# Row factors of an attention kernel spread over the partitions by transfers through DRAM instead of by matrix products

## What is computed

```python
h = jnp.einsum('bnd,ade->bane', feat_in, W)            # 12 heads of 32
th = jnp.tanh(h)
attn_src = jnp.einsum('bane,aeo->bano', th, w_src)     # s, one per row and head
attn_dst = jnp.einsum('bane,aeo->bano', th, w_dst)     # d, one per column and head
attn = attn_src + jnp.swapaxes(attn_dst, 2, 3)
attn = jnp.where(attn >= 0, attn, LEAKY_ALPHA * attn)  # 0.2
attn = jnp.where(~adj[:, None], -999.0, attn)
attn = jax.nn.softmax(attn, axis=-1)
feat_out = jnp.einsum('banm,bame->bane', attn, h) + b
feat_out = jax.nn.elu(feat_out)
gate = jax.nn.sigmoid(feat_in @ H_w.T + H_b)
return gate * feat_out + (1.0 - gate) * feat_in
```

## Time and profile before

| | before |
|---|---|
| median of 3 runs | 1105.98 us (1105.11 to 1106.05) |
| the profiled execution | 1105.45 us |
| its span | 1103.6 us |
| PE busy | 1056.6 us (96%), 9199 instructions |
| PEld busy | 895.9 us (81%) |
| DVE busy | 872.9 us (79%), 2289 instructions |
| POOL busy | 703.9 us (64%), 605 instructions |
| ACT busy | 651.4 us (59%), 2060 instructions |
| chain that ended last, by engine | PE 79%, DVE 12%, issue 6%, ACT 1% |
| DMA | 31.00 MB, mean 28 GB/s |

### The profile page before, as it was taken

One profiled execution on the slowest core, in us unless ns is written; L12 is line 12 of the kernel. 1 busy time (PEld: TensorE's weight loads), 2 busy tenths in 40 slices (PEclk: granted clock), 3 DMA queues, 4 the chain that ended last, 5 costly groups with the idle time before them and its releaser, 6 DMA issues.

```text
span 1103.6 us, 28424 instructions
## 1 busy us (share of the span) xinstructions
PE 1056.6 (96%) x9199; PEld 895.9 (81%) x9199; DVE 872.9 (79%) x2289; ACT 651.4 (59%) x2060; POOL 703.9 (64%) x605
## 2 busy tenths in 40 slices
PE   6999999999999999999999999999999999999964
PEld 4888888888888888888888888888888888888753
DVE  3659779696987969789696987969689796978986
ACT  4747466474755647565575746657565564747522
POOL 0347577575757758577574856757576674857764
PEclk9999999999999999999999999999999999999985
DMA  7101010010101001010100101001010100100000
GB/s 188 32 1 33 30 33 15 19 34 21 31 29 31 7 21 31 29 31 20 37 9 21 31 29 31 7 21 31 29 31 29 31 7 21 31 29 2 10 15 36
DMA packets 34722, 31.00 MB, mean 28 GB/s; under 512 B 15872, under 2 KB 34688, under 8 KB 34688
## 3 DMA queue, kind: packets, MB, share of 16 engines
q1 hardware_dynamic: 34688, 30.57, 9.1%
HBM read 17.98 MB, written 12.58 MB: 28 GB/s over the span
## 4 chain that ended last, share of the span: by engine, by line
PE 79%; DVE 12%; issue 6%; ACT 1%; POOL 0%; DMA 0%; DVEq 0%; POOLq 0%; ACTq 0%
PE p_bank L573 50%; PE t_bank L712 5%; PE context L726 5%; DVE weights L1032 4%; PE scores L635 4%; PE context L732 4%; PE t_bank L644 3%; PE context L656 3%; PE t_bank L605 2%; PE t_bank L740 2%; PE t_bank L682 2%; DVE sd L1001 1%; DVE masked L940 1%; DVE neg_max L948 1%; PE t_bank L703 1%
## 5 line engine op out<-in xcount | busy, mean ns | idle before, releaser
L1139 POOL TENSOR_TENSOR w_rows<-qwT,own_head 96x1536 fp32r<-96x1536 f32 x64 | 179.8, 2810 | 87.0 <-ACT qwT L873 87.0
L1032 DVE SCALAR_TENSOR_TENSOR weights<-t_bank,pqw,clip 128x128 f32<-128x128 f32 x768 | 206.4, 344 | 7.4 <-PE t_bank L712 6.6
L1132 POOL TENSOR_TENSOR prod<-th,w_sd 128x768 f32<-128x768 f32 x64 | 118.2, 1846 | 124.8 <-ACT th L836 124.7
L808 ACT ACTIVATE probs<-masked,neg_max 128x128 f32<-128x128 f32 x384 | 148.8, 391 | 46.4 <-DVE neg_max L948 46.4
L573 PE MATMUL p_bank<-xT,w_q 128*128 128x512 f32 x432 | 113.6, 408 | 4.3 <-DVE w_k L917 4.3
L573 PE MATMUL p_bank<-w_v,xT 128*128 128x384 f32 x576 | 115.2, 344 | 1.2 <-DVE clip L985 1.2
L573 PE MATMUL p_bank<-w_f,cT 128*128 128x384 f32 x576 | 115.4, 344 | 0.4 <-DVE cT L910 0.4
L573 PE MATMUL p_bank<-w_h,x1T 128*128 128x384 f32 x576 | 114.0, 343 | 0.2 <-DVE x1T L910 0.2
L573 PE MATMUL p_bank<-w_g,x1T 128*128 128x384 f32 x576 | 113.9, 342 | 0.0
L573 PE MATMUL p_bank<-xT,w_k 128*128 128x512 f32 x432 | 111.5, 402 | 0.0
L1120 POOL TENSOR_TENSOR probs<-probs,rden 128x768 f32<-128x768 f32 x64 | 94.3, 1473 | 25.2 <-DVE rden L953 25.2
(11 more groups left out here) (107 smaller groups left out, 2314.7 us busy)
## 6 DMA issues: line engine op xcount, KB each, us to landing
x_in<-in_x_dram SPq DMA_DIRECT2D x16, 768.0 KB, 4.7
out_dram<-y_out SPq DMA_DIRECT2D x64, 192.0 KB, 1.9
adj_in<-in_adj_dram SPq DMA_DIRECT2D x16, 64.0 KB, 4.3
probs0T<-in_L_gnn_Wq_dram SPq DMA_DIRECT2D x1, 576.0 KB, 5.7
weights<-in_L_gnn_Wk_dram SPq DMA_DIRECT2D x1, 576.0 KB, 6.8
x_res<-in_L_gnn_Wv_dram SPq DMA_DIRECT2D x1, 576.0 KB, 7.3
probs<-in_L_gnn_Wf_dram SPq DMA_DIRECT2D x1, 576.0 KB, 7.7
x<-in_L_gnn_W_dram SPq DMA_DIRECT2D x3, 192.0 KB, 6.1
```

What stands on the lines that cost most here:

```text
L808: last = act.activation(probs0[:, k % 2, b, j * P:(j + 1) * P], masked[:, k % 2, b * PAIRS + j, :], ACT.Exp, bias=neg_max[:, b * PAIRS + j ...
L1032: last = dve.scalar_tensor_tensor(out=weights[:, g % 2, n, :], in0=src[:, i * P:(i + 1) * P], scalar=pqw[:, g % 2, 0, n:n + 1], in1=clip[: ...
L1132: pool.tensor_tensor(prod[:], over_heads(th[:], 2), w_sd[:], ALU.mult).then_inc(s_prod, 1)
L1139: pool.tensor_tensor(w_rows[0:QW_ROWS, k % 2], over_heads(qwT[:, k % 2, 1, :].bitcast(F32), H1), per_head(own_head[:], P), ALU.mult).then_ ...
```

## The change

`qwhi`, `qwlo`, `qwT`, `qwTo` and `wb` go, and with them `qw_parts`, `qwT`, `own_head` and `w_rows`. ACT writes w to `w_exp` [128, 2, 12]. SP gets a list of its own with four kinds of steps. `keep` writes w_exp of a graph to a scratch in DRAM as [head, row]: 1536 words of 4 bytes, each its own piece, since neighbours in DRAM lie on different partitions. `spread` reads the scratch, 6 KB, once for each of the 128 partitions into `w_spread` [128, 12, 128]. Both are double buffered. `rows` on POOL now multiplies w_spread by q in place, and `e` reads w_spread instead of a PSUM bank. `load` and `store` are the other two kinds of steps on SP; load comes behind the first spread of a turn, the stores behind the last. PE is left with 22 instead of 38 uses of its transpose banks a turn. All lists of all engines are new in their order.

The diff, without most of the lists and the semaphores' declarations:

```diff
 PE_LOOP = [
-    ("v", 0), ("x1T", 0), ("qk", 0), ("x1T", 1), ("qk", 1), ("qk", 2), ("h", 0), ("gate", 0), ("qk", 3), ("h", 1),
-    ("qwT", 0), ("qk", 4), ("x1T", 2), ("qk", 5), ("gate", 1), ("s", 0), ("qwT", 1), ("wb", 0), ("v", 1), ("wb", 1),
-    ("s", 1), ("wb", 2), ("h", 2), ("wb", 3), ("wb", 4), ("pv1", 0), ("wb", 5), ("gate", 2), ("x1T", 3), ("sumsT", 0),
-    ("pv1", 1), ("h", 3), ("pT", 0), ("s", 2), ("pT", 1), ("pT", 2), ("pT", 3), ("pv0", 0), ("s", 3), ("qwT", 2),
-    ("sumsT", 1), ("v", 2), ("qwT", 3), ("f", 0), ("wb", 6), ("wb", 7), ("v", 3), ("wb", 8), ("pv0", 1), ("pT", 4),
-    ("pT", 5), ("wb", 9), ("wb", 10), ("pv1", 2), ("wb", 11), ("f", 1), ("sumsT", 2), ("pv0", 2), ("pT", 6),
-    ("maskT", 0), ("pv1", 3), ("maskT", 1), ("pT", 7), ("f", 2), ("sumsT", 3), ("pv0", 3), ("xT", 0), ("gate", 3),
-    ("xT", 1), ("f", 3), ("xT", 2), ("xT", 3),
+    ("qk", 0), ("qk", 1), ("x1T", 0), ("v", 0), ("qk", 2), ("x1T", 1), ("h", 0), ("gate", 0), ("x1T", 2), ("qk", 3),
+    ("h", 1), ("qk", 4), ("qk", 5), ("gate", 1), ("s", 0), ("v", 1), ("s", 1), ("h", 2), ("s", 2), ("gate", 2),
+    ("pv1", 0), ("x1T", 3), ("sumsT", 0), ("v", 2), ("pT", 0), ("pT", 1), ("h", 3), ("pv0", 0), ("pv1", 1), ("s", 3),
+    ("maskT", 0), ("v", 3), ("pT", 2), ("pT", 3), ("f", 0), ("xT", 0), ("pv0", 1), ("sumsT", 1), ("gate", 3),
+    ("pT", 4), ("pT", 5), ("f", 1), ("pv0", 2), ("xT", 1), ("pv1", 2), ("pT", 6), ("sumsT", 2), ("pT", 7), ("f", 2),
+    ("pv0", 3), ("xT", 2), ("xT", 3), ("pv1", 3), ("maskT", 1), ("sumsT", 3), ("f", 3),
 ]
...
 DVE_LOOP = [
-    ("x1lo", 0), ("gsum", 0), ("x1lo", 1), ("sd", 0), ("sda", 0), ("wlog", 0), ("qwlo", 0), ("sd", 1), ("sda", 1),
-    ("wlog", 1), ("qwlo", 1), ("gsum", 1), ("x1lo", 2), ("mask", 0), ("e", 0), ("max", 0), ("e", 1), ("e", 2),
-    ("mask", 1), ("e", 3), ("e", 4), ("e", 5), ("rden0", 0), ("max", 1), ("rden1", 0), ("x1lo", 3), ("f_raw", 0),
-    ("sd", 2), ("sda", 2), ("rden0", 1), ("wlog", 2), ("gsum", 2), ("mask", 2), ("max", 2), ("sd", 3), ("sda", 3),
-    ("qwlo", 2), ("wlog", 3), ("mixa", 0), ("mixb", 0), ("qwlo", 3), ("sum1", 0), ("rden1", 1), ("clo", 0),
-    ("stats1", 0), ("mask", 3), ("mv1", 0), ("rden0", 2), ("f_raw", 1), ("max", 3), ("e", 6), ("e", 7), ("e", 8),
...
+    ("x1lo", 0), ("gsum", 0), ("x1lo", 1), ("sd", 0), ("sda", 0), ("wlog", 0), ("sd", 1), ("sda", 1), ("wlog", 1),
+    ("gsum", 1), ("x1lo", 2), ("mask", 0), ("max", 0), ("mask", 1), ("e", 0), ("e", 1), ("e", 2), ("max", 1),
+    ("gsum", 2), ("sd", 2), ("rden0", 0), ("sda", 2), ("e", 3), ("rden1", 0), ("x1lo", 3), ("f_raw", 0), ("wlog", 2),
+    ("e", 4), ("rden0", 1), ("e", 5), ("mask", 2), ("max", 2), ("clo", 0), ("mixa", 0), ("mixb", 0), ("sum1", 0),
+    ("clip", 0), ("sd", 3), ("sda", 3), ("wlog", 3), ("rden0", 2), ("mask", 3), ("stats1", 0), ("max", 3),
+    ("sum0", 0), ("stats0", 0), ("mv1", 0), ("xlo", 0), ("mv0", 0), ("rden1", 1), ("clo", 1), ("f_raw", 1), ("e", 6),
...
 POOL_LOOP = [
-    ("prod", 0), ("prod", 1), ("rows", 0), ("rows", 1), ("x_res", 0), ("prod", 2), ("norm", 0), ("fb", 0),
-    ("norm", 1), ("prod", 3), ("ex", 0), ("rows", 2), ("norm", 2), ("rows", 3), ("fb", 1), ("norm", 3), ("ex", 1),
-    ("rstd1", 0), ("rstd0", 0), ("fb", 2), ("ex", 2), ("rstd0", 1), ("fb", 3), ("rstd1", 1), ("rstd0", 2), ("ex", 3),
-    ("rstd1", 2), ("rstd0", 3), ("rstd1", 3),
+    ("x_res", 0), ("prod", 0), ("prod", 1), ("rows", 0), ("prod", 2), ("rows", 1), ("norm", 0), ("fb", 0),
+    ("norm", 1), ("ex", 0), ("prod", 3), ("norm", 2), ("rows", 2), ("fb", 1), ("norm", 3), ("ex", 1), ("rows", 3),
+    ("rstd1", 0), ("rstd0", 0), ("fb", 2), ("ex", 2), ("rstd0", 1), ("rstd1", 1), ("fb", 3), ("rstd0", 2), ("ex", 3),
+    ("rstd0", 3), ("rstd1", 2), ("rstd1", 3),
 ]
...
+SP_LOOP = [
+    ("keep", 0), ("spread", 0), ("load", 0), ("keep", 1), ("spread", 1), ("keep", 2), ("spread", 2), ("keep", 3),
+    ("spread", 3), ("store", 0), ("store", 1), ("store", 2), ("store", 3),
+]
...
-SHIFT = {n: 2 for n in ("xT", "xhi", "xlo")} | {n: 1 for n in (
+SHIFT = {n: 2 for n in ("xT", "xhi", "xlo", "load")} | {n: 1 for n in (
...
-        pqw = sb("pqw", [P, 2, 3, H1])
-
-
-        qw_parts = sb("qw_parts", [P, 2, 2, QW_ROWS], F32R)
-        qwT = sb("qwT", [QW_ROWS, 2, 2, P], F32R)
-        own_head = sb("own_head", [QW_ROWS, H1])
-        w_rows = sb("w_rows", [P, 2, H1, P], F32R)
+        pq = sb("pq", [P, 2, 2, H1])
+
+
+        w_exp = sb("w_exp", [P, 2, H1])
+        w_kept = [nc.dram_tensor(f"w_kept{i}", [H1, P], F32, kind="Internal").ap() for i in range(2)]
+        w_spread = sb("w_spread", [P, 2, H1, P])
         weights = sb("weights", [P, 2, H1, P])
...
-            def load(t):
-                first = at(t * GROUP)
-
-                sp.wait_ge(pe["xT"], upto(t, GROUP, 0))
-                sp.wait_ge(s_xb, upto(t, 1, 0))
-                sp.wait_ge(s_adjb, upto(t, 1, 0))
-                sp.sem_inc(s_free, 1)
-                sp.dma_start(x_in[:], x_dram[:, bass.ds(first, GROUP), :]).then_inc(s_x, 16)
-                sp.dma_start(adj_in[:], adj_dram[:, bass.ds(first, GROUP), :]).then_inc(s_adj, 16)
-
-            def store(t):
-                for g in range(GROUP):
-                    graph = at(t * GROUP + g)
-                    sp.wait_ge(s_y, upto(t, GROUP, g + 1))
+            def step(name, k, g1, turn):
+                if name == "load":
+                    t = g1 + 2
+                    first = at(t * GROUP)
+
+                    sp.wait_ge(pe["xT"], upto(t, GROUP, 0))
+                    sp.wait_ge(s_xb, upto(t, 1, 0))
+                    sp.wait_ge(s_adjb, upto(t, 1, 0))
+                    sp.sem_inc(s_free, 1)
+                    sp.dma_start(x_in[:], x_dram[:, bass.ds(first, GROUP), :]).then_inc(s_x, 16)
+                    sp.dma_start(adj_in[:], adj_dram[:, bass.ds(first, GROUP), :]).then_inc(s_adj, 16)
+                elif name == "keep":
+
+                    sp.wait_ge(s_pqw, upto(g1, 3 * GROUP, 3 * k + 3))
+                    sp.sem_inc(s_spread_free, 1)
+
+                    wait(sp, s_wspread[k % 2], upto(g1, GROUP // 2 * 16, k // 2 * 16))
+                    sp.sem_inc(s_spread_free, 1)
+                    sp.dma_start(w_kept[k % 2].rearrange("h i -> i h"), w_exp[:, k % 2, :],
+                                 allow_slow_non_contiguous=True).then_inc(s_kept[k % 2], 16)
+                elif name == "spread":
+
+                    sp.wait_ge(s_kept[k % 2], upto(g1, GROUP // 2 * 16, (k // 2 + 1) * 16))
+                    sp.sem_inc(s_spread_free, 1)
+
+                    wait(sp, s_e, upto(g1, THIRDS * GROUP, THIRDS * (k - 1)))
+                    sp.sem_inc(s_spread_free, 1)
+                    sp.dma_start(w_spread[:, k % 2].rearrange("p h i -> p (h i)"),
+                                 w_kept[k % 2].rearrange("h i -> (h i)").partition_broadcast(P)
+                                 ).then_inc(s_wspread[k % 2], 16)
+                elif name == "store":
+                    graph = at(g1 * GROUP + k)
+                    sp.wait_ge(s_y, upto(g1, GROUP, k + 1))
                     sp.dma_start(out_dram[:, bass.ds(graph, 1), :],
-                                 y_out[:, g % 2, :].unsqueeze(1)).then_inc(s_store[g % 2], 16)
-
-            load(1)
-            load(2)
-            store(0)
-            with sp.Fori(1, NG - 2) as u:
-                load(u + 2)
-                store(u)
-            store(NG - 2)
-            store(NG - 1)
+                                 y_out[:, k % 2, :].unsqueeze(1)).then_inc(s_store[k % 2], 16)
+
+            phases(sp, step, "SP", NG)
             for g in range(2):
...
-                elif name == "qwT":
-
-                    te.wait_ge(s_qwlo, upto(g1, GROUP, k + 1))
-                    dst = bank(t_bank, t_freed, name, k, g1, turn)
-                    for i in range(2):
-                        last = te.transpose(dst[0:QW_ROWS, i * P:(i + 1) * P], qw_parts[:, k % 2, i, :].bitcast(F32),
-                                            ident[:])
-                    last.then_inc(pe["qwT"], 1)
-                elif name == "wb":
-
-                    g, r = divmod(k, THIRDS)
-                    te.wait_ge(s_rows, upto(g1, GROUP, g + 1))
-                    dst = bank(t_bank, t_freed, name, k, g1, turn)
-                    heads = slice(H1 // THIRDS * r, H1 // THIRDS * (r + 1))
-                    te.matmul(dst[:, :], qwT[:, g % 2, 0, :],
-                              w_rows[0:QW_ROWS, g % 2, heads, :].rearrange("p h i -> p (h i)"),
-                              start=True, stop=True).then_inc(pe["wb"], 1)
                 elif name == "pv1":
...
-                    wait(act, s_qwlo, upto(g1, GROUP, k - 1))
-                    act.activation(pqw[:, k % 2, 0, :], sda[:, 1, :], ACT.Exp).then_inc(s_pqw, 1)
-                    act.activation(pqw[:, k % 2, 1, :], sda[:, 1, :], ACT.Exp, scale=LEAKY).then_inc(s_pqw, 1)
+                    wait(act, s_prod1, upto(g1, GROUP, k - 1))
```

(54 more changed lines are left out.)

187 lines of the change are left out of this document (90 added, 97 removed), and 107 rows, old and new, of tables (DVE_BEGIN, DVE_END, DVE_LOOP, PE_BEGIN).

## The result

The changed kernel takes 1638.01 us (1628.96 to 1640.78, four runs) against 1105.55 us (1102.65 to 1106.05, four runs) of the kernel before: 1.481 times as long, 95% interval 1.4745 to 1.4875. The forecast was 1066, the range 1022 to 1122; even the case of slow transfers ended at 1132. The profiled run took 1640.78 us.

The account below looks back on a forecast made before the run. PE was taken to bound the loop: 65.8 us a turn less 5.4, plus 2.5 waiting, gives p = 62.9. With 242.0 for begin and end, 1029 + 15 (p - 60.4) gave 1066 us, range 1022 to 1122.

Parts of the forecast that it names:

- the case of slow transfers: Rival: keep and spread at their upper ends, 12.2 us together, turn 64.5, 1091 us, a loss above 13.2; chance 0.12.
- PE's loss of work, 60.4 us a turn: PE in the loop sheds 12 broadcasts (4.2 us) and 8 transposes (1.2), so its turn falls from 65.8 to 60.4 us.
- the case that all hides: Rival: transfers and port cost nothing, PE alone sets the turn at 60.4 us, 1029 us in all; chance 0.22.
- the open L: Begin and end: the transfer latency lies open in the last graph's chain, adding 5 us, for 242.0 in all.
- e at its old price: DVE's e, reading w_spread in SBUF instead of PSUM, stays at 12.8 us a turn.
- rows 2.8, spread 4.7: POOL's rows takes 2.8 us as before; the spread lands in 4.7 us, ends 3.9 and 6.1.
- keep 2.8, ends 1.9 and 6.1: The store of 1536 4-byte words lands in 2.8 us: fixed part about 1.4 plus 1.4 for the pieces.
- L once a turn: Latency from w's exponential to w on all partitions, 7.5 us, ends 5.8 and 12.2; up to about 8 little is lost.
- turn = 52.3 + L: Turn length once the latency from w's exponential to w on all partitions exceeds about 8 us.
- Load behind spread 0 is free: SP's load of x_in behind the first spread costs nothing, as x_in is wanted 25 us later.
- The port, 2.5 us on POOL: POOL's prod 2 waits for e 2 at the SBUF port; PE waits 2.5 us a turn at pT 0, 2.0 for the port.
- DVE pays: Rival: DVE stands still for POOL's operations, 12.8 us a turn, turn 66.6, 1122 us, slower; chance 0.16. Sign: e's mean longer.

Follow-up runs that it names:

- 18: Kernel after without keep and spread, e reading one constant SBUF tile, rows and x_res both cut to 12 columns: 1085.99 us (0.9836).
- 11: Kernel after without keep and spread, e reading one constant SBUF tile, rows cut to 12 columns: 1153.77 us.
- 10: Kernel after without keep and spread, rows multiplying a constant SBUF tile by q, e on one SBUF input: 1201.95 us (1.0895).
- 5: Kernel after without keep, spreads reading a scratch filled once, e as a reduction with one SBUF input: 1221.41 us (1.1055).
- 6: Kernel after with keep, e as a reduction with one SBUF input: 1598.10 us (1.4468).
- 2: Kernel after without keep, spreads reading a scratch filled once, e still on two SBUF inputs: 1416.92 us.
- 7: Kernel after with keep's 1536 words written 512 bytes apart, spreads reading another scratch filled once: 1364.62 us.
- 4: Kernel before with all of e reading a constant SBUF tile instead of PSUM: 1312.57 us (1.1887).
- 9: Kernel before with the middle one of each graph's three e steps reading a constant SBUF tile instead of PSUM: 1285.22 us (1.1649).
- 14: Kernel before with POOL's x_res moved in the loop from behind rows 1 to the head of its list: 1129.31 us (1.024).
- 1: Kernel after with scratch as [row, head], so keep writes 128 pieces of 48 bytes; rows and e read in 48-byte steps: 1478.39 us (1.3381).
- 16: Kernel after with SP issuing keeps in pairs, the second before the wait for the first to land: 1820.03 us (1.6494).
- 13: Kernel after without keep and spread, e on one SBUF input, x_res moved in the loop to behind prod 1: 1205.38 us (1.0914).

## Why the prediction was wrong, step by step

The sum of the prediction, 1066 us, is fast for four reasons: the keep was sized at 2.8 us and took 11.5; its latency was counted once a turn and stands three times in the chain; the port was charged to POOL and is paid by DVE; and the new place of x_res was not priced at all. The runs add up so: 1086 (18), with x_res 1154 (11), with rows 1202 (10), with the spread 1221 (5), with the keep 1598 (6), with e's second input 1638. The last two steps depend on their order: e's second input costs 196 us without a keep (2 and 5) and 40 with one.

- **PE's loss of work, 60.4 us a turn.** PE's own work came out near: busy 985 us in 18, forecast 970, and in its loop, from 500 to 600 us, 93.66 of 100 us at clock 1.00, which makes 61.0 us a turn. But no run came near the case that all hides, 1029: with even rows and x_res cut a turn is 65.1, and mix is still slowed in it. Whether 60.4 could be had without any fight for the port, no run shows. I had laid out the new order's path for one graph and took the rest as PE-bound. Begin and end went from 248 to 338 us; in 18, with no transfers, they take 237, which is what the sum had before its 5 for the open L.
- **e at its old price.** When POOL doesn't shut it out it costs less, 271 ns at the shortest against a mean of 344 before; with a mean of 511 this doesn't come to bear.
- **rows 2.8, spread 4.7**: 2.79 and 4.4. Right; 6.7 where the next keep is issued 1 us behind the spread, and 4.0 in 5, without keeps.
- **keep 2.8, ends 1.9 and 6.1**: 11.5 us. The term that failed worst. The rate of W's 1536 pieces is one of reads from DRAM, of 128 bytes each; I used it for writes of 4 bytes. The split of a store's 1.9 us that gave its fixed 1.4 is in no row either. The pieces do pass the engines within 2 us; the 9.5 us behind are in no row of before. The bound should have stayed open upwards, as the trace had no row of a small write. The Trainium skill (DMA: Bandwidth & Descriptors, Specifications) has a read-modify-write under 512 B. 7 against the kernel after shows that size alone is not it, since as many words of the same size, with room between them, land in 3.4 us.
- **L once a turn.** "SP is taken for 4 L, no queue grows" and "turn = 52.3 + L" failed. L is on the path three times for keep and twice for spread, by SP's order and by wlog 2 behind e 3. With the measured L = 15.9 the formula gives a turn of 68.2 and 1146 us; the turn is 100.1 and the time 1638. So the wrong size of the keep alone explains 80 of the 572 us by which the forecast was missed; the rest is in how often it counts, in the port and in x_res.
- **Load behind spread 0 is free**: no. The load's two issues, 1.4 us, stand in the chain before keep 1; keep 1, beside it, takes 12.5 us in place of 11.2; and x_in lands in 9.3 in place of 4.7.
- **The port, 2.5 us on POOL.** POOL's means did not move (prod 1854 ns, norm 1479), and e's rose to 511: the sign that I named for "DVE pays". That rival had the mechanism right. Its 12.8 us of work for DVE came near by luck (12.3 in 4), since its working, by shares, fails in 9; and it still took the time too low, as DVE's free time hid none of it in 4. I had left out that a DVE operation with one SBUF input is shut out too (y_out, wlog, x). The Trainium skill says it in the section I quoted (SBUF — State Buffer, Who interferes with whom): a `tensor_scalar` can use both port pairs, a `tensor_reduce` never contends. The traces agree: y_out 3.55 us, wlog 2.66, while the reductions sd and neg_max keep their 936 to 948 ns in the runs after as before. Its rule is that whoever issues first blocks the other. With pieces of 0.3 us on DVE and 1 to 3.5 on POOL, it would cost POOL little even if both waited as often; but in 9 DVE doesn't get in between two POOL operations either, and why is not shown.
- **Not in the sum at all**: x_res at the head of POOL's list (68 us between 18 and 11), though the diff shows it, and PE's clock. The same 8879 instructions keep PE busy 985 us at 0.988 (18), 1014 at 0.962 (10), 1123 at 0.85 (after). So a kernel in which PE waits long pays for it again in PE's clock; the short waits of 14 left the clock at 0.99.

## What to carry to other kernels

Before a product on PE is replaced by transfers, look for a row of just such a transfer, direction, piece and neighbourhood in DRAM; without one leave its bound open, and follow the chain through all graphs of a turn, counting how often the latency stands in it. When an operand moves from PSUM to SBUF, list every POOL operation that can be running or queued there; here the queue set the price, not the share of busy time, and moving one POOL operation only slowed other steps in its place. A list's order is part of the change even for steps that keep their work.

## What the runs showed of the hardware

- 1536 words of 4 bytes written next to each other in DRAM land 11.2 to 12.5 us after issue (medians of graphs 0 and 1), 768 of them in 9.1 to 12.4, and 1536 at a distance of 512 bytes in 3.4 (page of 7). SP waits 1.7 for 128 pieces of 48 bytes (1). A spread that lands in 4.0 us without keeps (5) took 13.9 beside one (16).
- An x_in load of 768 KB lands in 9.3 us beside such a keep, 5.0 without (5).
- A DVE operation of 12 columns with one SBUF input can take 2.66 us (wlog in 13). One with a PSUM and an SBUF input takes its usual time beside POOL: gate_sum 0.55 us at 597.77 in 13, inside rows' 597.48 to 600.23, and none of the 64 x1T over 0.56.
